# Four quarters of the array and a shorter ranking chain in the first attention of a two-layer transformer kernel

## The reference

```python
def _proj(W, b, x): return jnp.einsum('oi,bil->bol', W, x) + b[:, None]
q, k, v = _proj(Wq, bq, layernorm(x)), _proj(Wk, bk, ctx), _proj(Wv, bv, ctx)   # each 32 x 64 x 512
# 8 heads of 64 features; rows d and columns e are the 64 positions
scores = jnp.einsum('hbdk,hbek->hbde', qh, kh) / sqrt(64)
xh = jnp.einsum('hbde,hbek->hbdk', softmax(scores), vh)
x = x + _proj(Wo, bo, xh)
n = layernorm(x)
_, top = jax.lax.top_k(n @ W_gate + b_gate, 2)             # of 8 experts
x = x + mean over the two of relu(n @ W_e[top] + b_e[top])
# layer 2: attention with 32 heads of 16, then a gated feed-forward; unchanged here
```

## Time and profile before

| | us |
|---|---|
| median of three runs | 904.88 (904.84 to 909.71) |
| the profiled execution | 898.77 |
| its span, first to last instruction | 897.0 |
| PE busy | 855.2 (95%) |
| DVE busy | 439.6 (49%) |
| ACT busy | 346.7 (39%) |
| POOL busy | 291.4 (32%) |
| mean granted clock of PE | 0.987 |

### The profile page before, as it was taken

One profiled execution on the slowest core, in us unless ns is written; L12 is line 12 of the kernel. 1 busy time (PEld: TensorE's weight loads), 2 busy tenths in 40 slices (PEclk: granted clock), 3 DMA queues, 4 the chain that ended last, 5 costly groups with the idle time before them and its releaser, 6 DMA issues.

```text
span 897.0 us, 19708 instructions
## 1 busy us (share of the span) xinstructions
PE 855.2 (95%) x7537; PEld 697.0 (78%) x7537; DVE 439.6 (49%) x900; ACT 346.7 (39%) x567; POOL 291.4 (32%) x412
## 2 busy tenths in 40 slices
PE   5999999699999979999999899999999999999997
PEld 4788878588888857777777688878888788878885
DVE  4898877244444567888888732213222212122112
ACT  3655654233333356766666532321222122211110
POOL 4588876000000577777763231112020002002000
PEclk9999999799999989999999999999999999999999
DMA  8556666686553543554432431110030003001001
GB/s 290 176 199 240 224 208 226 240 282 237 166 165 127 180 147 83 161 159 134 136 80 58 135 106 48 48 33 0 13 118 12 1 12 106 1 30 65 0 1 47
DMA packets 55084, 105.24 MB, mean 117 GB/s; under 512 B 8050, under 2 KB 12146, under 8 KB 54866
## 3 DMA queue, kind: packets, MB, share of 16 engines
q1 hardware_dynamic: 48226, 84.98, 29.3%
q0 software_dynamic: 5120, 16.78, 5.8%
q10 hardware_dynamic: 1648, 2.23, 0.7%
HBM read 67.99 MB, written 35.98 MB: 116 GB/s over the span
## 4 chain that ended last, share of the span: by engine, by line
PE 75%; issue 2%; ACT 2%; DMA 1%; DVE 1%; POOL 1%; SPq 0%; DVEq 0%; ACTq 0%; POOLq 0%
PE c_ps L1237 9%; PE c_ps L1239 9%; PE c_ps L1238 9%; PE c_bank L1749 4%; PE c_bank L1275 3%; PE c_bank L1276 3%; PE c_bank L1281 3%; PE c_bank L1810 3%; PE c_bank L1750 3%; PE c_bank L1754 3%; PE c_ps L1785 2%; PE c_bank L985 2%; PE c_bank L986 2%; PE c_bank L991 2%; PE c_po L985 2%; PE c_po L986 2%
## 5 line engine op out<-in xcount | busy, mean ns | idle before, releaser
L1314 DVE SCALAR_TENSOR_TENSOR d_hid<-c_ps,d_b_up,d_silu 128x512 f32<-128x512 f32 (+1 forms) x44 | 33.0, 750 | 229.9 <-PE c_ps L1239 229.9
L1237 PE MATMUL c_ps<-d_nT_hi,gate_up_hi 128*128 128x512 f32 (+1 forms) x352 | 140.0, 398 | 0.0
L1239 PE MATMUL c_ps<-d_nT_hi,gate_up_lo 128*128 128x512 f32 (+1 forms) x352 | 138.7, 394 | 0.0
L1238 PE MATMUL c_ps<-d_nT_lo,gate_up_hi 128*128 128x512 f32 (+1 forms) x352 | 138.4, 393 | 0.0
L1193 ACT ACTIVATE d_silu<-c_ps,d_b_gate 128x512 f32<-128x512 f32 (+1 forms) x44 | 30.3, 688 | 141.6 <-PE c_ps L1239 141.6
L1153 POOL TENSOR_TENSOR late_x<-late_x,d_b_down 128x512 f32<-128x512 f32 x16 | 21.8, 1395 | 187.6 <-DMA late_x<-x_after_attention 187.6
L1239 PEld LDWEIGHTS c_ps<-d_nT_hi,gate_up_lo 128*128 128x128 f32 (+1 forms) x352 | 65.3, 185 | 16.5
L1238 PEld LDWEIGHTS c_ps<-d_nT_lo,gate_up_hi 128*128 128x128 f32 (+1 forms) x352 | 65.4, 186 | 15.8
L1237 PEld LDWEIGHTS c_ps<-d_nT_hi,gate_up_hi 128*128 128x128 f32 (+1 forms) x352 | 65.3, 186 | 15.3
L1200 ACT ACTIVATE d_hid_hi<-d_hid 128x512 fp32r<-128x512 f32 (+1 forms) x44 | 27.8, 632 | 126.0 <-DVE d_hid L1314 126.0
L1004 ACT ACTIVATE b_rowsT_hi<-c_bank 128x512 fp32r<-128x512 f32 x39 | 23.3, 599 | 85.4 <-PE c_bank L974 85.3
(11 more groups left out here) (297 smaller groups left out, 1959.3 us busy)
## 6 DMA issues: line engine op xcount, KB each, us to landing
b_rows<-expert_rows SPq DMA_DIRECT2D x39, 256.0 KB, 2.7
expert_results<-b_result SPq DMA_DIRECT2D x39, 256.0 KB, 2.5
a_wstage<-L_ffn_W_e SPq DMA_DIRECT2D x16, 512.0 KB
late_x<-x_after_attention SPq DMA_DIRECT2D x28, 256.0 KB, 4.0
c_stage<-gate_up SPq DMA_DIRECT2D x16, 344.0 KB, 3.4
out<-late_x SPq DMA_DIRECT2D x16, 256.0 KB, 2.8
x_after_attention<-late_x SPq DMA_DIRECT2D x12, 256.0 KB, 3.8
c_y_in<-x_after_attention SPq DMA_DIRECT2D x12, 256.0 KB, 2.8
```

Source lines behind the costliest of these rows:

```text
L1237: pe.matmul(bank[0:w, :], gu_hi[:, cols], nT_hi[:, g % 2, k, :], start=k == 0, stop=False)
L1238: pe.matmul(bank[0:w, :], gu_hi[:, cols], nT_lo[:, g % 2, k, :], start=False, stop=False)
L1239: mm = pe.matmul(bank[0:w, :], gu_lo[:, cols], nT_hi[:, g % 2, k, :], start=False, stop=k == KD - 1)
```

## The change

1. `make_scores` puts the result of batch element half r of head b at rows 64 (r xor b) and in bank b of a pair of banks (`pst`), so that four matmuls in a row use the four quarters of the array. DVE reads the scores of two banks and writes them in the order of heads that was there before. `ps` and `pt` are now the two banks of that pair, so the scores also wait until the transposed probabilities of the tile before are copied.
2. `make_attn` takes heads n and n+4 for both elements in turn, again in four quarters. Heads 4 to 7 come out with the two batch elements exchanged, so `project` becomes two matmuls of 256 columns, the second with `wo_cross`, whose two blocks lie off the diagonal. It costs one more memset and two more loads among the constants.
3. The start of the region is added by PE: `make_rank` has a third matmul, of one row of ones with `region_row`. DVE multiplies ranks and marks straight from PSUM, and the sum is written as whole numbers. The region addition, the sum of the marks over the tile, and the rounding are gone.
4. `seenb` now counts marks for each row, not for each expert over the tile (the matmul with ones sums over the rows anyway). POOL adds `both` to it for tiles 0 to 13, ahead of its low part and after the rank matmuls of that tile; DVE does it for tiles 14 and 15. POOL's wait for `both` ahead of the low part is gone.
5. DVE makes the marks after the shift of the scores. PE and ACT do the transposed x ahead of the values.

```diff
@@ -209,11 +208,13 @@
-    pk, pq, pvy, ps, pt, pr = (pb(n) for n in ("pk", "pq", "pvy", "ps", "pt", "pr"))
+    pst = stack.enter_context(nc.psum_tensor("a_pst", [P, 2, 512], F32))
+    ps, pt = pst[:, 0, :], pst[:, 1, :]
     po = stack.enter_context(nc.psum_tensor("a_po", [P, 2, 512], F32))
-    N_CONST = 13
+    N_CONST, SEEN_LATE = 14, 2
...
@@ -264,22 +265,21 @@
-    def group_ending(t):
-        return next((g for g, (first, n) in enumerate(GROUPS) if first + n - 1 == t), None)
-    def groups_until(t):
-        return sum(first + n <= t for first, n in GROUPS)
+    def add_seen(eng, t):
+        eng.wait_ge(r_made, t + 1)
+        want(eng, seen_ready, t)
+        eng.tensor_tensor(seenb[:, :], seenb[:, :], both[:, :], ALU.add).then_inc(seen_ready, 1)
     @block.sync
     def _(sp):
         def load_consts():
-            sp.wait_ge(zeroed, 4)
+            sp.wait_ge(zeroed, 5)
...
+            for half in range(2):
+                sp.dma_start(wo_cross[64 * half:64 * half + 64, 64 - 64 * half:128 - 64 * half], a["Wo"]).then_inc(o_consts, 16)
...
@@ -361,13 +361,13 @@
-        for buf in (wk, wv, wq, wo):
+        for buf in (wk, wv, wq, wo, wo_cross):
-        for buf, pattern, base in ((expert_no, [[1, 8]], 0), (region_at, [[REGION, 8]], P),
+        for buf, pattern, base in ((expert_no, [[1, 8]], 0), (region_at, [[REGION, 8]], P), (region_row, [[REGION, 8]], P),
...
@@ -424,9 +424,9 @@
                 scatter(m - 4)
             if m >= TILES - 1 and tile(m - 1):
                 scale_x1(m - 1)
+            if 0 <= m - 3 < TILES - SEEN_LATE:
+                add_seen(pool, m - 3)
             if tile(m - 1):
-                if tile(m - 3):
-                    pool.wait_ge(both_ready, groups_until(m - 2))
                 low_part(m - 1)
             if m < TILES - 1 and tile(m - 1):
                 scale_x1(m - 1)
...
@@ -504,10 +504,10 @@
                 high_part(m)
                 exponent(m)
                 keep_probT(m)
+            if tile(m - 2):
+                keep_xT(m - 2)
             if tile(m + 1):
                 keep_v(m + 1)
-            if tile(m - 2):
-                keep_xT(m - 2)
             if tile(m + 2):
                 norm_x(m + 2)
             if m == TILES - 1:
...
@@ -552,11 +552,13 @@
             pe.wait_ge(q_kept, t + 1)
             pe.wait_ge(k_kept, t + 1)
             want(pe, s_shifted, t)
+            want(pe, pt_kept, t)
             for j in range(4):
                 for b in range(2):
                     for r in range(2):
                         rows, cols = slice(64 * r, 64 * r + 64), slice(P * j + 64 * b, P * j + 64 * b + 64)
-                        mm = pe.matmul(ps[rows, cols], qT[rows, cols], kT[rows, cols], start=True, stop=True)
+                        at = 64 * (r ^ b)
+                        mm = pe.matmul(pst[at:at + 64, b, 64 * j:64 * j + 64], qT[rows, cols], kT[rows, cols], start=True, stop=True)
             mm.then_inc(s_made, 1)
         def transpose_probs(t):
...
@@ -570,22 +572,24 @@
             pe.wait_ge(pt_kept, t + 1)
             pe.wait_ge(v_kept, t + 1)
             want(pe, o_kept, t)
-            for h in range(H0):
-                for b in range(2):
-                    rows = slice(64 * b, 64 * b + 64)
-                    mm = pe.matmul(po[rows, h // 4, 65 * (h % 4):65 * (h % 4) + 65], probT[rows, 64 * h:64 * h + 64],
-                                   v[rows, t % 2, h, :], start=True, stop=True)
+            for n in range(H0 // 2):
+                for cross in range(2):
+                    for b in range(2):
+                        h, rows, at = n + 4 * cross, slice(64 * b, 64 * b + 64), 64 * (b ^ cross)
+                        mm = pe.matmul(po[at:at + 64, cross, 65 * n:65 * n + 65], probT[rows, 64 * (h ^ b):64 * (h ^ b) + 64],
+                                       v[rows, t % 2, h, :], start=True, stop=True)
             mm.then_inc(o_made, 1)
         def project(t):
             if t == 0:
-                pe.wait_ge(o_consts, 64)
+                pe.wait_ge(o_consts, 96)
             pe.wait_ge(o_kept, t + 1)
             if tile(t + 1):
                 pe.wait_ge(v_kept, t + 2)
             else:
                 pe.wait_ge(x1_ready, t)
-            pe.matmul(pvy[:, :], wo[:, :], attn[:, :], start=True, stop=True).then_inc(y_made, 1)
+            pe.matmul(pvy[:, 0:256], wo[:, :], attn[:, 0:256], start=True, stop=True)
+            pe.matmul(pvy[:, 256:512], wo_cross[:, :], attn[:, 256:512], start=True, stop=True).then_inc(y_made, 1)
         def transpose_x(t):
             pe.wait_ge(xn2_ready, t + 1)
...
@@ -603,23 +607,19 @@
                 pe.wait_ge(bg_split, 5)
             pe.wait_ge(xt_kept, t + 1)
             want(pe, found, t)
-            want(pe, ranked, groups_until(t))
+            want(pe, picked_ready, t)
             for i in range(3):
                 pe.matmul(pr[:, 0:8], ones[0:1, :], bg_parts[:, i, :], start=i == 0, stop=False)
             for j in range(4):
                 mm = pe.matmul(pr[:, 0:8], xT[:, P * j:P * j + P], wg[:, j, :], start=False, stop=j == 3)
             mm.then_inc(l_made, 1)
-        def make_rank(g):
-            first, n = GROUPS[g]
-            pe.wait_ge(both_ready, g + 1)
-            want(pe, seen_ready, g)
-            pe.matmul(pr[:, 0:8 * n], before[:, :], both[:, 0:n, :].rearrange("p t e -> p (t e)"), start=True, stop=False)
-            for i in range(n - 1):
-                pe.matmul(pr[:, 8 * i + 8:8 * n].rearrange("p (t e) -> p t e", e=8), ones[:, :],
-                          both[:, i:i + 1, :].to_broadcast([P, n - 1 - i, 8]), start=False, stop=False)
-            pe.matmul(pr[:, 0:8 * n].rearrange("p (t e) -> p t e", e=8), ones[:, :],
-                      seenb[:, :].rearrange("p (x e) -> p x e", x=1).to_broadcast([P, n, 8]), start=False, stop=True).then_inc(r_made, 1)
+        def make_rank(t):
+            pe.wait_ge(both_ready, t + 1)
+            pe.matmul(pr[:, 0:8], ones[0:1, :], region_row[0:1, :], start=True, stop=False)
+            pe.matmul(pr[:, 0:8], before[:, :], both[:, :], start=False, stop=False)
+            want(pe, seen_ready, t)
+            pe.matmul(pr[:, 0:8], ones[:, :], seenb[:, :], start=False, stop=True).then_inc(r_made, 1)
         def make_late_k(i):
             bank = kv_bank(i)
...
@@ -653,16 +653,16 @@
             if tile(m + 1):
                 make_k(m + 1)
                 make_q(m + 1)
-            if group_ending(m - 3) is not None and m < TILES:
-                make_rank(group_ending(m - 3))
+            if tile(m - 3) and m < TILES:
+                make_rank(m - 3)
             if tile(m):
                 transpose_probs(m)
+            if tile(m - 2):
+                transpose_x(m - 2)
             if tile(m + 1):
                 make_v(m + 1)
-            if tile(m - 2):
-                transpose_x(m - 2)
-            if group_ending(m - 3) is not None and m >= TILES:
-                make_rank(group_ending(m - 3))
+            if tile(m - 3) and m >= TILES:
+                make_rank(m - 3)
             if m == TILES - 1:
                 make_late_k(0)
             if m == TILES:
...
@@ -719,15 +719,18 @@
             want(dve, s_made, t)
             dve.tensor_tensor(by_position(qT[:, :]), by_position(pq[:, :]), every_bq, ALU.add).then_inc(q_kept, 1)
+        def all_scores():
+            return pst[:, :, 0:256].rearrange("p b (j e) -> p b j e", e=64)
         def max_scores(t):
             dve.wait_ge(s_made, t + 1)
-            dve.tensor_reduce(smax[:, :], ps[:, :].rearrange("p (g e) -> p g e", g=8), AX.X, ALU.max).then_inc(max_step, 1)
+            dve.tensor_reduce(smax[:, :].rearrange("p (b j) -> p b j", b=2), all_scores(), AX.X, ALU.max).then_inc(max_step, 1)
         def shift_scores(t):
             dve.wait_ge(max_step, t + 1)
             want(dve, pt_made, t)
-            peak = smax[:, :].rearrange("p (g x) -> p g x", x=1).to_broadcast([P, 8, 64])
-            dve.tensor_tensor(score[:, :].rearrange("p (g e) -> p g e", g=8), ps[:, :].rearrange("p (g e) -> p g e", g=8), peak, ALU.subtract).then_inc(s_shifted, 1)
+            peak = smax[:, :].rearrange("p (b j x) -> p b j x", b=2, x=1).to_broadcast([P, 2, 4, 64])
+            dve.tensor_tensor(score[:, :].rearrange("p (j b e) -> p b j e", b=2, e=64), all_scores(), peak, ALU.subtract).then_inc(s_shifted, 1)
         def heads():
             return po[:, :, 0:260].rearrange("p b (h l) -> p b h l", h=4)
...
@@ -766,43 +769,26 @@
...
+        def mark_experts(t):
+            dve.wait_ge(found, t + 1)
+            dve.tensor_tensor(hot_kept[:, t, :, :], chosen[:, t, 0:2].rearrange("p (k x) -> p k x", x=1).to_broadcast([P, 2, 8]),
+                              expert_no[:, :].rearrange("p (x e) -> p x e", x=1).to_broadcast([P, 2, 8]), ALU.is_equal).then_inc(hot_ready, 1)
+        def add_marks(t):
+            dve.wait_ge(hot_ready, t + 1)
+            want(dve, r_made, t)
+            want(dve, seen_ready, t)
```

(29 more changed lines are left out.)

56 lines of the change are left out of this document (12 added, 44 removed).

## The result

| | kernel before | changed kernel |
|---|---|---|
| median, us (20 runs each, one chip) | 906.06 | 912.23 |
| ratio, 95% interval | | 1.0072 (1.0056 to 1.0088) |
| again on another chip (e13) | 899.38 | 910.07, ratio 1.0120 (1.0094 to 1.0147) |
| profiled execution (span) | 898.77 (897.0) | 917.75 (915.9); in e13 span 907.9 |

The forecast was 905.4, 898 to 911. The change costs 6.2 us where I forecast 0.5, and 10.7 on the second chip.

What follows compares the result with a forecast made beforehand. POOL, at 8.16 us a tile, was taken to bound the first attention and absorb PE's saving. Start +1.2, up to the last transpose +0.0, end -0.7 gave +0.5 on the 904.88 median: 905.4 us, range 898 to 911.

Steps and rivals of the forecast that it cites:

- Quarters, 0.44 saved per group: PE's scores, and likewise attention, in four array quarters: 0.63 us instead of 1.07, 0.88 a tile for both.
- Rival 3: PE's quarters don't overlap and it keeps 7.96 + 0.05 us a tile: 908.6 us in all; chance 0.12.
- POOL's period as the bound that takes the saving: POOL's tile grows from 7.89 to 8.16 us and stays the bound; PE's saved 0.88 turns into waiting.
- The count: POOL's new 128x8 addition of marks: 0.20 us and 0.07 for handing over, 0.27 a tile.
- The moments up to the last transpose: Times summed along the first attention, ending with the last transpose of probabilities at 135.7 + 1.2 us, against 135.67.
- The 3.35 in the sum: PE's time from tile 3's scores to the rank matmuls: 3.82 us less the 0.44 of the scores.
- No wait of POOL for the rank matmuls from tile 3 on: POOL's subtractions come 8.16 us apart from tile 3 on, with no wait for PE ahead of the new addition.
- The region product, 0.03: The third rank matmul on PE, adding the region's start, costs 0.03 us a tile.
- PE alone: PE's tile without waits for other engines: 7.96 - 0.88 + 0.05 = 7.13 us.
- Behind it PE works on alone to 160: it saves one attention ... -0.7: After the last transpose of probabilities, PE saves one attention (0.44 us) and its wait for the count falls by 0.25.
- Rival 1: PE's saving comes through in full: -12.4 us, 892.5 us in all; chance 0.07.
- Rival 2: A ring of rank matmuls, count, subtraction, weight load, rounding, exponent, transpose decides if loads exceed 4.6 us: 909.3 us; chance 0.14.

Runs made afterwards that it cites:

- e13: The changed kernel again, as it is, on another chip: 910.07 us against 899.38 for the kernel before, ratio 1.0120.
- e1: The changed kernel with scores, attention and projection as in the kernel before, without the wo_cross loads; the new ranking stays: ratio 1.0132 to the kernel before.
- e12: Changed kernel, count behind low part, wo_cross loads late, weights three ahead, a quarter of each low part moved from POOL to DVE: ratio 0.9967 to kernel before.
- e2: The kernel before with the quarters alone (scores, attention, projection, wo_cross and its two loads), ranking as it was: ratio 1.0059 to the kernel before.
- e4: The changed kernel with the two wo_cross loads moved behind the second weights load in SyncE's queue: ratio 1.0069 to the kernel before.
- e14: The changed kernel with the first late K issued behind the logits of tile 13, not ahead of the last attention: ratio 1.0063 to the kernel before.
- e7: The changed kernel with expert weights loaded into their low part's place, three loads under way instead of two: ratio 0.9944 to the kernel before.
- e3: The changed kernel with POOL's count of marks added behind the low part, not ahead of it: ratio 1.0050 to the kernel before.
- e6: The changed kernel with the count behind the low part and the wo_cross loads behind the second weights load: ratio 1.0032 to the kernel before.

## Why the prediction was wrong

- **Quarters, 0.44 saved per group.** Right: 0.63 as worked out. Rival 3, by which they would gain nothing, is out; how much of it the second PSUM bank gives isn't shown.
- **POOL's period as the bound that takes the saving.** Right in kind; the size was 8.03 to 8.05, not 8.16. The count was priced at 0.27 and costs 0.15, since what follows it starts 0.15 after it.
- **The moments up to the last transpose.** I had the low part of tile 12 at 121.7 and the last transpose at 136.9; e13 has 121.89 and 137.19. Two errors cancel: nine periods are 1.0 shorter, and tile 3 comes at 49.5, 1.2 later than the 48.3 of the text. (The 3.35 in the sum, from the scores to the rank matmuls, is 3.38 by its own terms, and 3.48 in the trace.) The first profile's 142.9 has stalls of DVE in it that no row explains.
- **No wait of POOL for the rank matmuls from tile 3 on.** Wrong. The one at tile 2 was in the sum (low part at 40.1; e13 has 41.14, behind a wait of 3.9). Four more in the first trace add up to 5.0 us. e13 has one, 0.91, at tile 13, where it holds back the last slice of weights and the late loads behind it.
- **The region product, 0.03.** Wrong: 0.2 to 0.4 us a tile of PE (8.17 and 8.35 in e1, against 7.96), hidden as long as PE idles. So PE alone is not at 7.13 either; where it catches up without a wait in e12 its scores are 7.28 apart (69.69 to 76.97).
- **"Behind it PE works on alone to 160: it saves one attention ... -0.7".** This is the step that failed. The tail became 7 us longer. I had priced PE's own work in it and neither of two things: that PE needs at its first late K a load that stands in SyncE's queue behind the weights of tile 15, which wait for POOL; and that idle time, here and in the iteration ahead, lets its clock fall, so that the same matmuls take twice as long. In e13 the first is 2.6 us and the second 4.4. The kernel before reached that K at 136.60, with the second load there since 136.01, and did not have to wait; in e13 it lands at 140.69. A PE that is faster by 0.88 a tile, in a pipeline that isn't, hardly arrives earlier (1.4 us at the last transpose of e2); it arrives with idle time, and that has a price of its own.
- **Rivals.** Rival 1 (a gain) is out. Rival 2 had the right neighbourhood, the load of weights behind the low part, but not the place: the steady stretch doesn't suffer from it, the last slice and what is queued behind it do. In single tiles its ring shows (8.77 in e4, 8.73 in e14).

Left open: where e4 and e14 have their gain, since one profile of each shows it only in part; the 2.4 us behind the phase; which of PE's short waits let the clock fall; and the stalls of DVE marked "remote".

## What to carry to other kernels

When an engine that is only just the bound is made faster, don't price its idle time at nothing. Look where the idle time falls, whether the engine's clock depends on being busy, and which load the engine meets first at the end of the pipelined stretch: that is where the new slack turned into 7 us of loss. And follow every queue to its last entries. One more buffer changed nothing in the steady tile, but let the last slice, and what stood behind it, go out 7 us sooner, and turned a loss of 0.7% into a gain of 0.6% (e7; with two more moves, on the other chips, 1.2% into a gain of 0.3%). When operations are moved between engines, look also at which ones now run side by side: with the count moved, POOL's long subtraction met small operations of DVE, and each of the four meetings cost about 2 us or more.

## What the runs showed of the hardware

- 32 records of 64 x 64 in four quarters of the array, with the results in two banks by turns, take 0.63 us, in two quarters 1.07, though two of the four share their rows.
- A matmul with one row, ahead of small ones with 128, costs PE 0.2 to 0.4 us, 0.1 of it ahead of itself; the small ones cost 0.03 each.
- The clock fell at 139.0 in e13, with PE idle for 0.86, 0.78 and the first 0.7 of a wait of 2.47. It stayed at half for 10.2 us, which cost 4.4. In e14 it fell behind waits of no more than 0.97 and 0.72.
- GpSimd's 128x8 addition shows 0.20 and holds up the next operation by 0.15.
- Small additions and comparisons of DVE with both operands in SBUF took 2.08 to 2.90 us instead of 0.17 beside a long subtraction of GpSimd, four times (e3, e6, twice in e12), each ending 0.03 to 0.04 after it.
- Two loads of 256 KB, issued 0.5 apart, landed 4.6 to 5.3 us (the first) and 5.8 to 7.9 us (the second) after their issue in the seven traces in which PE waited for them.
